# A transformer layer on one core: deviations inverted in pairs, the first unit's scores in the projection, and extra products in attention's lead

## The chip, the cores and the metric

The kernel runs on one core of a Trainium2 chip. The metric is the time of one execution in microseconds (us), the median of several runs. Every time of the trace comes from one profiled execution; positions in it are us from the start of its span. TensorE is PE (its weight loads PEld), VectorE DVE, ScalarE ACT, GpSimd POOL and SyncE SP.

## What is computed

The reference is one pre-norm layer on x of shape (8, 512, 256), in float32:

```python
x = x + attn(layernorm(x))          # 16 heads of 16, scores + relative position bias, softmax
x = x + ffn(layernorm(x))
def ffn(x, ...):
    sh = gelu(xf @ sw1 + sb1) @ sw2 + sb2                 # shared expert, all rows
    logits = xf @ gate_w.T + expert_bias                  # 7 routed experts
    topv, topi = top_k(logits, 2); w = softmax(topv)      # two experts for each row
    h = gelu(einsum('td,edh->eth', xf, rw1) + rb1)
    out_e = einsum('eth,ehd->etd', h, rw2) + rb2
    return sh + einsum('te,etd->td', combine, out_e)
```

## The kernel before

The work stands in three stages, each with a program written out by hand for every engine; the engines meet only at semaphores, and each does its own work strictly in the order written.

**Projection** (`project`, L264). For each of the 8 batches, a slot: PE makes q and k in four groups (pQ, L508, each product in three parts of high and low halves), turns the next batch (pT, L498) and makes v (pV, L519); ACT copies the high half of a group (L459), DVE subtracts it for the low half (L426); SP stores q, k and v to DRAM (L549, L555). After the slots of batches 2 to 5, SP loads one of four tables of the near bias (`near`, L208), and at the very end the first of the attention units (`load_step` of quad 0, place 0: 11 transfers, L229 to L242).

**Attention** (`attend`, L643). A unit is four heads of one batch; there are 32, and a ring of four holds their q and k. For a unit, PE makes 16 blocks of scores (pS, L887, eight steps of two), DVE adds the bias to each and takes the negated maxima (L810, 0.61 us from start to start when it runs without a gap), and turns them (`turn`, L817 to L823). POOL stores the maxima to DRAM and loads them back as rows of q_st (L769, L776). Then PE makes the exponents with bias and maxima in the product (pE, L904, L912), ACT takes Exp (L847), and PE multiplies with the values (pC, L926). Scores run ahead of exponents by one unit and LEAD = 7 steps, so that a lead of 15 steps (L946) stands ahead of the first exponents, on PE alone; from step 1 of the first unit's exponents on, scores of the third unit are asked for. SP loads unit 1, the near bias as bands, then units 2 and 3 (L685 to L689), while ACT's queue stores batch 7 of the projection (L857 to L859).

**Routing and experts** (`finish`, L962). For batch i of 8: PE makes the gate's product (L1632), DVE chooses two experts for a row (`choose`, L1228 on), PE counts the rows before each (`rank`, L1645) and DVE works out the places (`slots`, L1305); POOL scatters the normalised rows to DRAM, 8 indirect transfers for each batch (L1184). Beside it runs the second layernorm of later batches: DVE multiplies the context with the inverse denominators (`context`, L580), PE projects it (`out_projection`, L603), DVE adds the residual and takes statistics (`add_residual`, L613 to L622), POOL inverts the deviation (`invert_deviation`, eight small instructions L256 to L634, for one batch of 4 values in a partition), ACT normalises into `xr` (L1503), PE turns the rows (L1625), ACT copies them (L1511). The shared expert (L1678, L1696) and the splitting of the experts' weights into high and low parts (`weights_hi` L1494, `weights_lo` L1207) fill in. When all rows are scattered, 38 tiles of 256 rows go through their experts (L1706, L1722, L1733), and the results are gathered and added.

```python
for i in range(B):                      # POOL, L1188
    if 2 <= i + 1 < B:
        inverse_deviation(i + 1)
    if i >= 1:
        scatter(i - 1, 1)
    scatter(i, 0)
```

## Time and profile before

| what | us |
|---|---|
| median of 3 runs | 822.09 (820.17 to 823.49) |
| the profiled execution, its own time | 820.95 |
| its span | 819.1 |
| PE busy in the span | 773.4 (94%) |
| PEld busy | 551.9 (67%) |
| DVE busy | 619.1 (76%) |
| ACT busy | 474.8 (58%) |
| POOL busy | 260.6 (32%) |
| granted TensorE clock, mean | 0.958 of full speed |

The span divides by PE's lines: projection to 101.5, attention to about 532, routing to about 661, expert tiles to about 785, and the end. Busy shares are means over stages with different limits; a matmul's end is modelled, so that a busy PE isn't PE at its peak. The granted clock is a share of full speed: 1.00 is 2.4 GHz, 0.50 is 1.2 GHz.

### The profile page before, as it was taken

To read this page: it belongs to the slowest core of one execution; us is meant where nothing else is said; L and a number is where in the kernel's file an instruction comes from. 1 tells how busy PE (TensorE), PEld (TensorE's weight loads), DVE (VectorE), ACT (ScalarE), POOL (GpSimd) and SP (SyncE) were. 2 spreads that over 40 slices of the span, in tenths; PEclk is the share of its full clock that TensorE was granted. 3 is DMA by queue.
4 is the path that set the end of the run, shared out by engine and by line. 5 is a ranking of instruction groups with operands and counts; after the bars stand their busy time and mean duration, and the time that the engine had idled before them with its cause. 6 is when DMAs were issued, how large, how long until landed. Compare 5 with 4: busy or idle time off the path is not lost. (4 is left out here: it accounts for less than half of the span.)

```text
span 819.1 us, 18303 instructions
## 1 busy us (share of the span) xinstructions
PE 773.4 (94%) x6261; PEld 551.9 (67%) x6261; DVE 619.1 (76%) x1928; ACT 474.8 (58%) x716; POOL 260.6 (32%) x407
## 2 busy tenths in 40 slices
PE   4899989999999999999999999998997999999997
PEld 2677737566566566566565665777765589999974
DVE  4666487889889889888888884477865567777966
ACT  2344404766766766666666667466454267777730
POOL 1222111121121111111111111237777526666650
PEclk9999956999999999999999999988897999999999
DMA  4899883553364343453345284466632545556769
GB/s 117 229 351 360 304 259 109 135 145 100 101 170 137 116 123 106 151 169 101 99 121 152 81 267 136 166 187 206 212 101 85 175 133 165 161 158 208 222 202 355
DMA packets 74763, 140.77 MB, mean 172 GB/s; under 512 B 14651, under 2 KB 34771, under 8 KB 74497
## 3 DMA queue, kind: packets, MB, share of 16 engines
q1 hardware_dynamic: 62996, 116.12, 46.1%
q0 software_dynamic: 9792, 19.54, 7.4%
q10 hardware_dynamic: 1884, 3.97, 1.4%
q8 instruction: 50, 0.82, 0.4%
q14 instruction: 41, 0.33, 0.1%
HBM read 85.71 MB, written 56.78 MB: 174 GB/s over the span
## 5 line engine op out<-in xcount | busy, mean ns | idle before, releaser
L810 DVE CUSTOM_DVE_ANT_0 sums<-pS,near 128x512 bf16<-128x512 f32 x512 | 329.4, 688 | 48.4 <-PE pS L887 40.0
L847 ACT ACTIVATE prob<-pE 128x1024 f32<-128x1024 f32 x256 | 248.6, 1022 | 152.9 <-PE pE L912 152.8
L912 PEld LDWEIGHTS pE<-bandT,place 64*128 64x128 f32 x2048 | 167.4, 190 | 12.6
L912 PE MATMUL pE<-bandT,place 64*128 64x244 f32 (+2 forms) x2048 | 164.4, 272 | 0.0
L887 PE MATMUL pS<-k_st,q_st 48*128 48x512 f32 x512 | 139.0, 478 | 6.1 <-DVE nmax L810 2.5
L887 PEld LDWEIGHTS pS<-k_st,q_st 48*128 48x128 f32 x512 | 62.8, 193 | 115.6 <-DVE nmax L810 87.8
L926 PE MATMUL pC<-prob,v_aug 128*32 128x512 f32 x1024 | 135.7, 604 | 0.0
L904 PE MATMUL pE<-q_st,k_st 62*128 62x512 f32 x512 | 115.7, 407 | 1.4 <-issue 1.4
L1199 POOL DMA_INDIRECT expert_rows<-rb,xr x76 | 83.7, 1101 | 57.1 <-DVE rb L1414 45.5
L1184 POOL DMA_INDIRECT routed_rows<-xr,slot_i x64 | 66.2, 1034 | 32.2 <-issue 31.3
L1733 PE MATMUL pD<-w2p,hT 128*128 x456 | 63.5, 289 | 0.4 <-DVE hT L1407 0.4
L776 POOL DMA_DIRECT2D q_st<-negated_maxima x64 | 34.9, 550 | 89.9 <-DMA negated_maxima<-turned 89.9
L904 PEld LDWEIGHTS pE<-q_st,k_st 62*128 62x128 f32 x512 | 57.7, 189 | 6.9 <-ACT prob L847 4.2
L785 POOL COPY v_aug<-v_raw 128x256 f32<-128x256 f32 x32 | 12.7, 398 | 151.3 <-PE pC L926 151.3
L1733 PEld LDWEIGHTS pD<-w2p,hT 128*128 128x128 f32 x456 | 56.8, 190 | 0.7 <-issue 0.6
L769 POOL DMA_DIRECT2D negated_maxima<-turned x32 | 22.6, 706 | 92.3 <-DVE turned L823 88.2
L508 PE MATMUL pQ<-xT,w_p 128*128 128x512 f32 x192 | 48.9, 405 | 3.2 <-DVE qk L426 2.5
L1407 DVE TENSOR_TENSOR hT<-ctx_sb,hT 128x512 fp32r<-128x512 f32 x38 | 26.3, 693 | 28.3 <-ACT hT L1560 28.3
L508 PEld LDWEIGHTS pQ<-xT,w_p 128*128 128x128 f32 x192 | 35.7, 193 | 15.5 <-DVE qk L426 6.5
L810 DVE DVE_READ_ACCUMULATOR2_ANT nmax<- 128x1 f32 x512 | 42.7, 83 | 0.0
L926 PEld LDWEIGHTS pC<-prob,v_aug 128*32 128x32 f32 x1024 | 20.4, 108 | 31.2 <-issue 30.4
L459 ACT ACTIVATE qk<-pQ 128x512 fp32r<-128x512 f32 x32 | 19.2, 599 | 31.6 <-PE pQ L508 27.3
(202 smaller groups left out, 1066.7 us busy)
## 6 DMA issues: line engine op xcount, KB each, us to landing
xr<-routed_rows SPq DMA_DIRECT2D x38, 258.0 KB, 2.9
q_st<-q_parts SPq DMA_DIRECT2D x64, 128.0 KB, 2.7
k_st<-k_parts SPq DMA_DIRECT2D x64, 128.0 KB, 2.9
ctx<-ctx_sb SPq DMA_DIRECT2D x32, 256.0 KB, 2.7
q_parts<-qk SPq DMA_DIRECT2D x14, 512.0 KB, 7.8
k_parts<-qk SPq DMA_DIRECT2D x14, 512.0 KB, 7.4
near<-bias_by_distance SPq DMA_DIRECT2D x16, 448.0 KB, 5.0
xr<-expert_rows SPq DMA_DIRECT2D x14, 512.0 KB, 4.3
```

What stands on the lines that cost most here:

```text
L508: ins = pe.matmul(pQ[:, m % 2], w_p[:, a, w, c, P * h:P * h + P], xT[:, par, z, c], start=k == 0, stop=k == 5)
L776: pool.dma_start(raw(q_st[row:row + KM, m % RING]), max_dram[m].rearrange("a (p h) s -> h a p s", h=2)[side]).then_inc(max_ld, 16)
L810: dve.tensor_tensor_reduce(sums[:, r % 4], pS[:, unit % PS], near[:, hg % 2, j, lead:lead + S], -1.0, BIG, ALU.add, ALU.min, nmax[:, j, t: ...
L847: act.activation(prob[:, par, 2 * step:2 * step + 2], pE[:, 2 * (step % 2):2 * (step % 2) + 2], ACT.Exp).then_inc(exp_done, 1)
L887: pe.matmul(pS[:, unit % PS], q_st[rows, r, pair, P * t:P * t + P], k_st[rows, r, pair], start=True, stop=True).then_inc(s_mm, 1)
L904: pe.matmul(pE[:, bank + side], k_st[rows, r, pair, P * t:P * t + P], q_st[rows, r, pair], start=True, stop=False, skip_group_check=True)
L912: ins = pe.matmul(pE[:, bank + side, a:z], place[rows, half], bandT[rows, (quad // 2) % 2, pair, part, lead:lead + z - a], start=False, st ...
L926: ins = pe.matmul(pC[32 * j:32 * j + 32], v_aug[:, par, t, j], prob[:, par, at], start=t == 0, stop=t == TT - 1, skip_group_check=True)
L1184: pool.indirect_dma_start(xs_dram[:, :], bass.IndirectOffsetOnAxis(ap=slot_i[:, b, c, t:t + 1], axis=0), xr[:, b % XR, t, c], None).then_i ...
L1199: pool.indirect_dma_start(yc_dram[:, :], bass.IndirectOffsetOnAxis(ap=place_of, axis=0), y_rows(i)[:, t], None).then_inc(y_out[i % NXG], 16)
L1407: dve.tensor_tensor(hT[:, i % 2, 1], h_f[:, i % 2], hT[:, i % 2, 0], ALU.subtract).then_inc(s["hlo"], 1)
L1733: ins = pe.matmul(pD[:, i % 2, t], hT[:, i % 2, a, TS * m + P * t:TS * m + P * t + P], w2p[:, bass.ds(expert, 1), z, m].rearrange("p a n - ...
```

## The change

It has three parts. In the projection, the tables of the near bias are loaded one slot earlier (after batches 1 to 4), unit 0 is loaded after batch 5's stores and unit 1 at the end, both before attention begins. In the last slot, batch 7's, PE makes the 16 blocks of unit 0's scores between its own groups, two at a time, into the two banks of pB, and DVE takes their maxima between the low halves and after them. Attention then starts with `turn(0)` on DVE, and PE's lead has seven steps, each followed by two products of `ident` with itself into pC, which nobody reads. In the routing, one inversion serves two batches (2 and 3, 4 and 5, 6 and 7), at every second batch and between two halves of a scatter; the out projections, residuals, contexts and parts of the weights are done in pairs too, and in other places of the engines' orders.

```diff
-        mv = sb("mv2", [P, TT, 2], F32)
-        half = sb("half2", [P, TT], F32)
-        rtmp = sb("rtmp2", [P, 2, TT], F32)
-        rstd = sb("rstd2", [P, 2, TT], F32)
-        nbias = sb("nbias", [P, 2, TT], F32)
+        mv = sb("mv2", [P, 2, TT, 2], F32)
+        half = sb("half2", [P, 2, TT], F32)
+        rtmp = sb("rtmp2", [P, 2, 2, TT], F32)
+        rstd = sb("rstd2", [P, 4, TT], F32)
+        nbias = sb("nbias", [P, 4, TT], F32)
...
                 for b in range(B - 1):
                     slot(b, b % 2, b // 2, b < B - 2)
                     if b < 2:
                         load_rows(b)
-                    elif b < 2 + HPG:
-                        if b == 2:
-                            wait_apart(sp, passed, bias_stored, 16 * (4 + FARS))
-                        loads["near"](sp, 0, b - 2)
-                for m in range(4):
-                    wait_apart(sp, passed, qk_out[m], 16 * (B - 2))
-                wait_apart(sp, passed, v_out, 16 * (B - 2))
-                loads["step"](sp, 0, 0, True)
+                    if b == 1:
+                        wait_apart(sp, passed, bias_stored, 16 * (4 + FARS))
+                    if 1 <= b < 1 + HPG:
+                        loads["near"](sp, 0, b - 1)
+                    if b == 1 + HPG:
+                        stored(B - 4)
+                        loads["step"](sp, 0, 0, True)
+                stored(B - 2)
+                loads["step"](sp, 0, 1, True)
...
+                        if not one:
+                            maxima(m)
...
+                def maxima(step):
+                    pair, t = divmod(step, TT)
+                    for side in range(2):
+                        unit, j = 2 * step + side, 2 * pair + side
+                        if t == 0:
+                            dve.wait_ge(g["near_ld"][j], 16)
+                        dve.wait_ge(g["s_mm"], unit + 1)
+                        if unit >= 4:
+                            dve.wait_ge(g["max_done"], unit - 3)
+                        lead = P * t
+                        dve.tensor_tensor_reduce(g["sums"][:, unit % 4], pB[:, unit % 2], g["near"][:, 0, j, lead:lead + S], -1.0, BIG,
+                                                 ALU.add, ALU.min, g["nmax"][:, j, t:t + 1]).then_inc(g["max_done"], 1)
...
+                for step in range(4, 2 * TT):
+                    maxima(step)
...
+                def scores(step):
+                    pair, t = divmod(step, TT)
+                    if step == 0:
+                        pe.wait_ge(g["qk_ld"][0], 16 * 8)
+                        pe.wait_ge(bias_done, 2)
+                    for side in range(2):
+                        unit = 2 * step + side
+                        rows = slice(HALF * side, HALF * side + KQ)
+                        if unit >= 2:
+                            pe.wait_ge(g["max_done"], unit - 1)
+                        pe.matmul(pB[:, unit % 2], g["q_st"][rows, 0, pair, P * t:P * t + P], k_st[rows, 0, pair],
+                                  start=True, stop=True).then_inc(g["s_mm"], 1)
...
+                            scores(m)
...
+                            if u == 1:
+                                ins.then_inc(v_mm, 1)
+                            if not one:
+                                scores(4 + t)
...
+def inverses_until(b):
+
+    return b + 1 if b < 2 else 2 + b // 2
...
+        dve.wait_ge(s["var2"], 4 * b)
+    if b >= 2:
+        dve.wait_ge(s["rstd2d"], inverses_until(b - 2))
...
-def invert_deviation(pool, g, b):
-
-    s, mv, rstd, nbias = g["early"], g["mv"], g["rstd"][:, b % 2], g["nbias"][:, b % 2]
-    pool.wait_ge(s["var2"], 4 * b + 4)
-    _, ins = rsqrt_steps(pool, g["passed"], mv, g["half"][:], rstd, g["rtmp"], s["chain2"], 7 * b)
+def invert_deviation(pool, g, batches):
+
+    s, b, count = g["early"], batches[0], 7 * (inverses_until(batches[0]) - 1)
+    part, rows = slice(b % 2, b % 2 + len(batches)), slice(b % 4, b % 4 + len(batches))
+    mv, rstd, nbias = g["mv"][:, part], g["rstd"][:, rows], g["nbias"][:, rows]
+    half, tmp = g["half"][:, part], g["rtmp"]
+    pool.wait_ge(s["var2"], 4 * batches[-1] + 4)
+    _, ins = rsqrt_steps(pool, g["passed"], mv, half, rstd, tmp[:, :, part], s["chain2"], count)
     ins.then_inc(s["chain2"], 1)
-    pool.wait_ge(s["chain2"], 7 * b + 6)
-    pool.tensor_tensor(nbias, mv[:, :, 0], rstd, ALU.mult).then_inc(s["chain2"], 1)
-    pool.wait_ge(s["chain2"], 7 * b + 7)
+    pool.wait_ge(s["chain2"], count + 6)
+    pool.tensor_tensor(nbias, mv[:, :, :, 0], rstd, ALU.mult).then_inc(s["chain2"], 1)
...
-                loads["step"](sp, 0, 1, True)
...
+                turn(0)
+                for ahead in range(STEPS, STEPS * NI):
...
-                for step in range(STEPS + LEAD):
-                    scores(step // STEPS, step // STEPS, 1, step % STEPS)
+                for step in range(LEAD):
+                    scores(1, 1, 1, step)
+                    for _ in range(2):
+                        pe.matmul(pC[:, 0:P], g["ident"][:], g["ident"][:], start=True, stop=True)
...
-                    if i + 4 < B:
-                        sp.wait_ge(s["wo_mm"], 2 * (i + 2) + 2)
-                        load_context(sp, g, i + 4)
+                    for b in (i + 4, i + 5):
+                        if i % 2 == 0 and b < B:
+                            sp.wait_ge(s["wo_mm"], 2 * (b - 2) + 2)
+                            load_context(sp, g, b)
...
-                def inverse_deviation(b):
-                    pool.wait_ge(s["xn2"], 4 * (b - 2) + 4)
-                    invert_deviation(pool, g, b)
-
-                def scatter(b, c):
+                def inverse_deviations(pair):
+                    if pair[0] >= 4:
+                        pool.wait_ge(s["xn2"], 4 * (pair[0] - 3) + 4)
+                    invert_deviation(pool, g, pair)
+
+                def scatter(b, c, tokens=range(TT)):
                     if b == 0:
                         pool.wait_ge(pad_out[1], 16)
                     pool.wait_ge(s["slot_done"], b + 1)
                     pool.wait_ge(s["meta_done"], 2 * b + 2)
                     pool.wait_ge(s["xn2"], 4 * b + 4)
-                    for t in range(TT):
+                    for t in tokens:
                         pool.indirect_dma_start(
                             xs_dram[:, :], bass.IndirectOffsetOnAxis(ap=slot_i[:, b, c, t:t + 1], axis=0),
                             xr[:, b % XR, t, c], None).then_inc(scat[b % XR], 16)
 
                 for i in range(B):
-                    if 2 <= i + 1 < B:
-                        inverse_deviation(i + 1)
-                    if i >= 1:
+                    if i % 2 == 1 and i + 2 < B:
+                        scatter(i - 1, 1, range(2))
+                        inverse_deviations((i + 1, i + 2))
+                        scatter(i - 1, 1, range(2, TT))
+                    elif i >= 1:
                         scatter(i - 1, 1)
...
+                context(dve, g, 3)
                 dve.wait_ge(s["consts"], 7 + NE)
                 for i in range(B):
-                    if 1 <= i < B - 1:
-                        residual(i + 1)
-                    if i >= 3 and i % 2 == 1:
-                        add((i - 3) // 2)
                     choose(i)
-                    if i < B - 1:
-                        shares_and_places(i)
                     if i == 0:
                         dve.wait_ge(s["den_ld"], 16)
                         dve.reciprocal(den[:], den[:]).then_inc(s["den_inv"], 1)
-                    if i < B - 1:
-                        running(i)
-                        slots(i)
-                    else:
-                        running(i)
-                        slots(i)
-                        shares_and_places(i)
-                    if i + 3 < B:
-                        context(dve, g, i + 3)
-                    if i < NR:
-                        for k in (2 * i, 2 * i + 1):
+                    running(i)
+                    slots(i)
+                    shares_and_places(i)
+                    if i % 2 == 0:
+                        for b in (i + 2, i + 3):
+                            if b < B:
+                                residual(b)
+                    elif i >= 3:
+                        add((i - 3) // 2)
+                    rounded = (2 * i - 2, 2 * i - 1, 2 * i, 2 * i + 1) if i % 2 == 1 else (2 * i, 2 * i + 1)
+                    if i in (1, 3, 5, NR - 1):
+                        for k in rounded:
                             weights_lo(k)
+                    if i % 2 == 1:
+                        for b in (i + 3, i + 4):
+                            if b < B:
+                                context(dve, g, b)
...
-                        act.wait_ge(s["rstd2d"], b + 1)
+                        act.wait_ge(s["rstd2d"], inverses_until(b))
...
                         normalise(i + 1, 0)
+                    if i + 1 < B:
+                        turned(i + 1)
                     if i % 2 == 1:
                         shares(i // 2)
-                    if i + 1 < B:
-                        turned(i + 1)
                     if i < NR:
                         for k in (2 * i, 2 * i + 1):
...
                     if i % 2 == 1:
                         shared_up(i // 2, 0)
                         shared_up(i // 2, 1)
-                        if i < B - 1:
-                            turn_shares(i // 2)
-                    elif i >= 2:
-                        shared_down(i // 2 - 1, (0,))
-                    if i + 2 < B:
-                        out_projection(i + 2)
+                    else:
+                        if i >= 2:
+                            shared_down(i // 2 - 1, (0,))
+                        if i + 2 < B:
+                            out_projection(i + 2)
                     rank(i)
                     if i + 1 < B:
                         turn_rows(i + 1)
-                    if i % 2 == 0 and i >= 2:
-                        shared_down(i // 2 - 1, (1,))
+                    if i % 2 == 1:
+                        if i < B - 1:
+                            turn_shares(i // 2)
+                    else:
+                        if i >= 2:
+                            shared_down(i // 2 - 1, (1,))
+                        if i + 3 < B:
+                            out_projection(i + 3)
                 turn_shares(EARLY)
                 pe.wait_ge(s["tab_chain"], 3 * B)
                 pe.matmul(pX[:, 1, 0, 0:2 * NE], ones_b[:], cum[:, B], start=True, stop=True).then_inc(s["cnt_mm"], 1)
```

How the orders change shows at three places. PE, from the last slots of the projection to the first exponents (pQ and pV are the projection's, pB and pS scores, pC the values' bank, pE exponents; L5.. lines of `project`, L8.. or L9.. of `attend`). Before:

```order
L519 MATMUL pV<-w_p,xT 128x256 x24
L508 MATMUL pQ<-xT,w_p 128x512 x24
L519 MATMUL pV<-w_p,xT 128x256 x24
L308 UNCONDITIONAL_BRANCH
L873 UNCONDITIONAL_BRANCH
L887 MATMUL pS<-k_st,q_st 128x512 x32
L904 MATMUL pE<-q_st,k_st 128x512 x2
```

The 16 blocks of unit 0 and 16 of the later ones stand in one run behind the projection (30 of the lead and 2 of the first step). Now:

```order
L561 MATMUL pV<-w_p,xT 128x256 x24
L548 MATMUL pQ<-xT,w_p 128x512 x6
L538 MATMUL pB<-k_st,q_st 128x512 x2
...
L561 MATMUL pV<-w_p,xT 128x256 x6
L538 MATMUL pB<-k_st,q_st 128x512 x2
L312 UNCONDITIONAL_BRANCH
L927 UNCONDITIONAL_BRANCH
L941 MATMUL pS<-k_st,q_st 128x512 x2
L1003 MATMUL pC<-ident 128x128 x2
...
L941 MATMUL pS<-k_st,q_st 128x512 x2
L958 MATMUL pE<-q_st,k_st 128x512 x2
```

Unit 0's blocks went into the last slot, a pair behind each of its eight groups (four of pQ, four of pV), and seven pairs with the extra products are what is left of the lead.

POOL, from the first scatters of the routing on (L256 to L634, now L260 to L689, are one inversion). Before:

```order
L1184 DMA routed_rows<-xr,slot_i 60928x258 x4
L256 TENSOR_SCALAR rtmp<-mv 128x4
L257 TENSOR_TENSOR rstd<-rtmp,half 128x4
L258 TENSOR_TENSOR rtmp<-rstd 128x4
L259 TENSOR_TENSOR rtmp<-rtmp 128x4
L260 TENSOR_SCALAR rtmp<-rtmp 128x4
L261 TENSOR_TENSOR rstd<-rstd,rtmp 128x4
L632 TENSOR_TENSOR nbias<-mv,rstd 128x4
L634 TENSOR_SCALAR nbias<-nbias 128x4
L1184 DMA routed_rows<-xr,slot_i 60928x258 x8
```

An inversion of 4 values stands ahead of every 8 scatters, six times. Now:

```order
L1242 DMA routed_rows<-xr,slot_i 60928x258 x6
L260 TENSOR_SCALAR rtmp<-mv 128x8
L261 TENSOR_TENSOR rstd<-rtmp,half 128x8
L262 TENSOR_TENSOR rtmp<-rstd 128x8
L263 TENSOR_TENSOR rtmp<-rtmp 128x8
L264 TENSOR_SCALAR rtmp<-rtmp 128x8
L265 TENSOR_TENSOR rstd<-rstd,rtmp 128x8
L687 TENSOR_TENSOR nbias<-mv,rstd 128x8
L689 TENSOR_SCALAR nbias<-nbias 128x8
L1242 DMA routed_rows<-xr,slot_i 60928x258 x16
```

Three inversions of 8 values are left, with 16 scatters from one to the next.

PE, from batch 2's gate to batch 3's (gate into pX from ga_f, shared expert's second product into pD, out projection from wo_f, counting from mask, turning from xr). Before:

```order
L1632 MATMUL pX<-ga_f,x2T 128x7 x8
L1694 MATMUL pD<-b2s,cTs 128x256
...
L603 MATMUL pX<-wo_f,cn 128x256 x8
L1645 MATMUL pX<-mask,tri_b 128x64
...
L1625 MATMUL pX<-ident,xr 128x128 x8
L1694 MATMUL pD<-b2s,cTs 128x256
...
L1632 MATMUL pX<-ga_f,x2T 128x7 x8
```

Each batch has one out projection ahead of its count. Now:

```order
L1692 MATMUL pX<-ga_f,x2T 128x7 x8
L1754 MATMUL pD<-b2s,cTs 128x256
...
L648 MATMUL pX<-wo_f,cn 128x256 x8
L1705 MATMUL pX<-mask,tri_b 128x64
...
L1685 MATMUL pX<-ident,xr 128x128 x8
L1754 MATMUL pD<-b2s,cTs 128x256
...
L648 MATMUL pX<-wo_f,cn 128x256 x8
L1692 MATMUL pX<-ga_f,x2T 128x7 x8
```

An even batch has two, and the second stands last, ahead of the next batch's gate; an odd batch has none.

## Rows read from the trace of the kernel before

**Rows 1.** Windows: busy us of each engine (count), granted clock, DMA share, GB/s.

```profile
84.00:88.00 4.00, 3.94 (x18) 2.88 (x17) 2.17 (x7) 1.72 (x3) 2.07 (x6) 1.00 1.08 382
132.00:136.00 4.00, 3.83 (x24) 3.22 (x24) 2.32 (x7) 1.83 (x3) 0.00 (x0) 0.54 0.01 4
544.74:651.00 106.26, 95.89 (x420) 69.32 (x420) 75.28 (x368) 51.96 (x103) 80.63 (x112) 0.86 0.51 158
```

**Rows 2.** Timeline of attention's lead: start, us, engine, line, instruction [idle before <-releaser].

```profile
102.80 0.70 PE L887 MATMUL pS<-k_st,q_st 48*128 48x512 f32 x3 [1.24 <-DVEq L796]
...
113.20 0.08 DVE L810 DVE_READ_ACCUMULATOR2_ANT nmax<- 128x1 f32 x1
...
114.57 0.97 POOL L769 DMA_DIRECT2D negated_maxima<-turned  x1 [10.85 <-DVE turned L823]
...
114.59 1.22 PE L887 MATMUL pS<-k_st,q_st 48*128 48x512 f32 x3 [2.30 <-DMA k_st<-k_parts]
```

**Rows 3.** PE's timeline from the first exponents on.

```profile
123.72 1.01 PE L904 MATMUL pE<-q_st,k_st 62*128 62x512 f32 x2
...
126.41 0.64 PE L887 MATMUL pS<-k_st,q_st 48*128 48x512 f32 x1
...
136.19 0.49 PE L887 MATMUL pS<-k_st,q_st 48*128 48x512 f32 x1 [0.36 <-DVE nmax L810]
...
138.85 0.49 PE L887 MATMUL pS<-k_st,q_st 48*128 48x512 f32 x1 [0.33 <-DVE nmax L810]
```

**Rows 4.** Timeline of the projection's last two slots, SP's queue and ACT.

```profile
85.76 1.72 SPq L549 DMA_DIRECT2D q_parts<-qk  x2
...
94.03 0.64 SPq L229 DMA_DIRECT2D q_st<-q_parts  x1
...
94.24 0.60 ACT L459 ACTIVATE qk<-pQ 128x512 fp32r<-128x512 f32 x1 [0.79 <-PE pQ L508]
...
100.69 0.35 SPq L242 DMA_DIRECT2D v_raw<-v_rows  x1
```

**Rows 5.** Line L549, the stores of q and k.

```profile
DMA to landing us min/median/max: 3.2/7.1/8.4
```

**Rows 6.** Timeline of POOL, the inversion for batch 6 between two scatters, and the last wait.

```profile
591.48 0.96 POOL L1184 DMA_INDIRECT routed_rows<-xr,slot_i  x1 [0.30 <-issue]
...
592.85 1.04 POOL L257 TENSOR_TENSOR rstd<-rtmp,half 128x4 f32<-128x4 f32 x1
...
596.12 1.10 POOL L1184 DMA_INDIRECT routed_rows<-xr,slot_i  x1 [0.51 <-issue]
...
641.44 0.96 POOL L1184 DMA_INDIRECT routed_rows<-xr,slot_i  x1 [1.55 <-issue]
```

**Rows 7.** Timeline of DVE and PE in the routing.

```profile
535.87 6.68 PE L603 MATMUL pX<-wo_f,cn 128*128 128x256 f32 x16
...
587.06 1.28 DVE L613 TENSOR_TENSOR x1c<-pX,x1c 128x512 f32<-128x512 f32 x2
...
597.45 1.22 DVE L580 TENSOR_TENSOR cn<-cn,rb 128x1024 f32<-128x1024 f32 x1
...
599.12 1.13 PE L1696 MATMUL pD<-w_sh,ctx_sb 128*128 128x256 f32 x4
...
600.72 0.69 DVE L1207 TENSOR_TENSOR w2p<-wst,w2p 128x512 fp32r<-128x512 f32 x1
...
608.81 4.00 PE L603 MATMUL pX<-wo_f,cn 128*128 128x256 f32 x16
...
619.77 0.15 DVE L1228 TENSOR_TENSOR logits<-pX,eb 128x28 f32<-128x28 f32 x1
...
624.73 0.17 DVE L1313 CAST slot_i<-slot_f 128x8 int32<-128x8 f32 x1
```

**Rows 8.** Chain that ended last, in order of time: start, us, what.

```profile
650.87 4.52 DMA routed_rows<-xr,slot_i
...
660.94 0.66 PE pX L1706 x4
```

30 lines of the change are left out of this document (18 added, 12 removed).

## Prediction

> **What bounds the kernel now.** I read the windows first, for the clock and for the engine that is never free; then the timeline of attention's lead and of the projection's last slots; then POOL's timeline and the chain of waits in the routing. The windows show two weak places. At 132 to 136 PE is granted 0.54 of its clock, though attention has long begun, and in the routing, from 544.7 to 651, it has 0.86 on average [rows 1]. In the same 106.3 us POOL is busy for 80.6, more than its neighbour DVE (75.3), and what is left is mostly a gap of 0.30 that stands ahead of each scatter [rows 1, 6]: POOL sets the pace. The chain says the same: from the last scatter at 650.87 it goes through the DMA to PE's first tiles at 660.94 [rows 8]. In the lead the order is: first scores at 102.80, the last maximum of unit 0 at 113.20, its store to DRAM at 114.57, PE's wait of 2.30 for unit 1's k until 114.59, the first exponents at 123.72 [rows 2, 3]. In between, attention has nothing for ACT and little for PE. The steady part of attention (to about 530) and the expert tiles (from 661) are PE's; the change doesn't touch them, so what is won ahead of them shifts them whole.
>
> **Part 1: unit 0's scores in the last slot of the projection.** Nothing is removed: 16 blocks go from the lead into batch 7's slot. DVE carries it. It gets its first low half there at about 94.9, behind ACT's copy at 94.24 [rows 4]; from then on it has four low halves (a subtraction of 128x512 takes 0.69 [rows 7]) and 16 maxima at a cadence of 0.61 (16 of them fill most of 102.80 to 113.28 [rows 2]), so 2.8 + 9.8 = 12.6 us: 107.5. PE feeds it with two banks instead of three and has to make its own groups between; I add 1 us: 108.5. Between stages PE stood idle for about 1.3 before 102.80 [rows 2]; so `turn(0)` comes at 109.8 instead of behind 113.28: 3.5 us earlier. PE's part is hidden by DVE's: 16 blocks of 512 columns beside some 9 us of its own groups.
>
> What the moved load does to SP's queue: unit 0's eleven transfers, issued from 94.03 to 101.04 [rows 4], now stand from about 84 to 91, ahead of the stores of batch 6's q and k, which before were issued from 85.76. These become about 5 us late. Batch 7's first copy overwrites a buffer that such a store reads; it ran at 94.24, and a store takes 7.1 us to land in the median, 3.2 at least [rows 4, 5]. So 91.1 plus 3.2 to 7.1 gives 94.3 to 98.2: a stall of 0 to 4 us in the last slot. The DMA engines are full there (share 1.08 [rows 1]), but unit 0's megabyte replaces a table of the near bias, and I take 1 us. The Trainium skill ("Trainium Kernel Development and Optimization", Key Constraints) says that transfers issued from SP, ACT and POOL all run on the same 16 engines and interleave. By that rule the early load delays the stores even on another queue; it is the fourth case below. The tables of the near bias, each one slot earlier, cost nothing: the number in front of loads of x stays about the same.
>
> Unit 1 is now loaded by about 105, in the projection, so the wait of 2.30 and the 1.3 until the first block's maximum go, and the lead is 14 blocks: 110.8 + 0.7 for `turn` + 8.5 = 120. Late next is unit 2, which PE asks for one step behind the first exponents (126.41 before [rows 3]). Its transfers stand at attention's start, behind the bands, beside batch 7's stores on ACT's queue. Unit 1 stood just so before and took from about 102.5 to 114.59, 12.1 us [rows 2]; from 110.8 that gives 122.9, at which PE goes on instead of at 126.4. **Part 1 is worth -3** (ends: 0, where the stall is 4; -5.5, where neither costs).
>
> **Part 2: the products that nobody reads.** 14 products of 128 columns, on PE alone, and PE waits there for DVE: cover is DVE's 1.22 per pair of blocks. At full clock an out product of 256 columns is two records, 4.00/16 = 0.25 each [rows 7], so one of these is at most 0.5 us; two of them and two blocks fit 1.22 about exactly. At the low clock they don't, and the lead grows by at most 0.6 per step, 4 us in all. What they can bring: the first three pairs of steps, from 123.72 to 136.19, took 12.5 us, 4.16 each, at about half of the clock (0.54 at 132 to 136) [rows 1, 3]; the next pair, at full clock, took 2.66 [rows 3]. Held at 2.4 GHz they save 4.5 us. PE had fallen behind two gaps and a stretch in which it had one block in 0.61 us. Now it is busy in most of each step, but the gap between the stages stays, with nothing in it. I take that the clock falls there and is back within the lead or by the first pair: **-3** (ends: -4.5 and +1.5, where it stays low and the products lengthen the lead).
>
> **Part 3: the routing.** An inversion costs POOL 596.12 - 591.48 - 1.27 (a scatter with its gap) = 3.4 us [rows 6]. Six are 20.4. A paired one runs the same eight instructions on 8 values. The pow takes 1.04 on 4 [rows 6]; on 8 it takes 1.04 to 2.08. I take 1.8, as a slow function on so little data is nearer to work than to overhead: 4.2 an inversion, three are 12.6. -7.8 for the three. (64 scatters of 1.27, the six inversions and the last wait make 103.0 of the 106.3; the other 3.3 are scatters that took longer, 0.05 each.) The wait of 1.55 at 641.44 [rows 6], for the shares of the last batch behind ACT and PE, goes with it, as DVE will be well ahead of POOL by then: -1.3. POOL's own bound is so -9.1. The Trainium skill ("GPSIMD Engine Reference", Performance versus the Vector engine) gives 2.6 cycles per element and core for two inputs. By that rule four more values cost nothing that shows, and the bound would be 2.3 lower, -11.4; the row of 1.04 for 4 values already speaks against taking it for the pow.
>
> But the pair ties the engines into a longer round. Statistics of batch i+3 (i even) release the inversion; then normalising, turning, copying, and the weights' parts, which were 601.4 - 595.6 = 5.8 after an inversion's end [rows 6, 7]; the copy of the shares, 0.6, now lies inside; then the second context of the pair, 1.2 [rows 7]; then PE: out projection 4.0, count 0.3, turning 1.1, half of the shared expert 2.7 (two of 1.37), out projection 4.0 = 12.1 [rows 7], during which DVE does choosing and places (624.9 - 619.8 = 5.1) and one residual (1.3 and 1.8 of statistics); last the second half's residual and statistics, 2.4 [rows 7]. 4.2 + 0.3 + 5.8 + 0.6 + 1.2 + 12.1 + 2.4 = 26.6 us for two batches, beside 25.3 of POOL's (16 x 1.32 + 4.2) and 27.9 before (16 x 1.32 + 6.8). The first such statistics, of batch 3, come when the second out projection of batch 0 is done: 535.87 + 6.68 [rows 7], 1.5 for count and turning, a wait of 1.8 for the first residual, 4.0, 2.4: 552.3. Two rounds later it is 605.5 for batch 7; then 4.2 of inversion and 26 scatters of 1.32: 644.0, against 651.8 before. The rounds need full clock. PE will stand idle in each for about 3 us behind an odd batch's shared expert, where it waits for the inversion; what idleness can cost shows at 535.87, behind the stage's change: 6.68 for an out projection instead of 4.00 [rows 7]. I give each round 1.5 us for it: 647.0. **Part 3 is worth -5** (ends: -9, or -11 by the skill's rule; 0, where a round takes 30.5). Weights and contexts in pairs cost DVE nothing new; SP's loads of weights 4 to 7 wait for the parts of batch 1 until about 561, and are wanted from 570. After the last scatter, PE's own rest ended at about 659.7 and DMA released the first tiles; both move, PE's by more, as its program of the eight batches ends earlier.
>
> **Sum.** -3 - 3 - 5 = -11 on the profiled execution's 820.95: 809.95. The median of the runs is 1.1 higher: **811.0**.
>
> **Rivals.** (a) The forecast, 805 to 815: 0.58. (b) The rounds take 29 to 31, since PE runs at 1.2 GHz in half of them; part 3 brings -3 to +1, the lead's -6 stays: 815. For it: 0.86 in the routing [rows 1]. Against: POOL's gap. 0.16. (c) POOL's bound is met, the clock is held and no stall comes: -4.5 - 4.5 - 9 = -18: 804. 0.10. (d) The change doesn't do what it says in the lead: stores of batch 6 late by 4, the clock falls at the stage's change and the products lengthen the lead; 0 + 1.5, and part 3 with -4: 819.5. 0.12. (e) Slower, by one mechanism: the clock in the rounds. If PE is at 1.2 GHz for all of them, two out projections cost 2 x 2.7 more, and half of the shared expert up to 2.7: 34.7 a round, and the last scatters end at 605.5 + 2 x 8.1 + 38.5 = 660.2, 8.4 later than before; with a lead that brings -2 that is +6.4: 828.5. It decides once a round is over 31. Against: rows of the routing show both lengths. 0.04.
>
> A measurement of this kernel can tell about 0.5%, 4 us, from no change. Faster by more than that (below 818): (a), (b), (c) and a little of (d), 0.85; within it 0.11; slower 0.04. The range is 803 to 819.
>
> **What would show it.** Right: the first exponents by 120 and PE past unit 2's first scores by 123; the clock at 1.00 in the pairs behind them; three inversions of about 4.2; scatters ending near 647; batch 7's first copy no later than 97. Wrong: exponents at 123 or later, a second stretch at 0.5 in the lead, POOL waiting for statistics by more than 4 us in a round.

## The result and the profile after

The change made the kernel slower: 830.71 us in the median of 20 runs (826.18 to 834.09) beside 823.28 (818.09 to 830.06) for the kernel before, a ratio of 1.009 with a 95% interval of 1.0069 to 1.0111. The forecast was 811.0, with 803 to 819 as its range. Runs of either kernel differ by 8 to 12 us among themselves, which will matter below.

The profiled execution took 829.28 us, 8.33 more than the one before. Two marks divide it: the first gate product of the routing (L1692 after, L1632 before) and PE's turning of the first expert tile (L1766, L1706).

| stretch | before | after | difference | forecast |
|---|---|---|---|---|
| span's start to first gate | 533.70 | 535.39 | +1.7 | -6 |
| first gate to first tile | 125.9 | 133.1 | +7.2 | -5 |
| first tile to the end | 159.5 | 158.8 | -0.7 | 0 |

**The lead.** Windows of the changed kernel, with the columns of [rows 1]:

```profile
107.00:112.00 5.00, 3.94 (x18) 2.43 (x17) 4.08 (x14) 1.15 (x2) 0.00 (x0) 1.00 0.00 2
112.00:117.00 5.00, 4.51 (x17) 3.07 (x18) 3.68 (x12) 0.00 (x0) 1.99 (x4) 0.68 0.77 250
117.00:122.00 5.00, 5.00 (x18) 3.01 (x17) 3.35 (x12) 0.00 (x0) 1.53 (x3) 0.50 1.05 356
122.00:127.00 5.00, 4.72 (x20) 3.29 (x20) 3.84 (x11) 0.00 (x0) 0.00 (x0) 0.50 1.00 220
...
132.00:137.00 5.00, 4.63 (x33) 4.09 (x32) 2.53 (x8) 2.69 (x3) 1.50 (x3) 0.50 0.72 162
137.00:142.00 5.00, 4.18 (x43) 3.33 (x41) 4.13 (x13) 3.35 (x4) 0.00 (x0) 0.93 0.07 16
```

And its timeline, which answers to [rows 2, 3]:

```profile
96.76 0.69 DVE L436 SCALAR_TENSOR_TENSOR qk<-pQ,qk 128x512 fp32r<-128x512 f32 x1 [3.40 <-ACT qk L486]
...
111.17 0.69 DVE L455 CUSTOM_DVE_ANT_0 sums<-pB,near 128x512 bf16<-128x512 f32 x1
...
112.16 4.70 SPq L218 DMA_DIRECT2D bandT<-bias_parts_by_distance  x4
...
112.49 0.51 PE L941 MATMUL pS<-k_st,q_st 48*128 48x512 f32 x2 [1.55 <-DVEq L849]
...
113.73 0.96 POOL L822 DMA_DIRECT2D negated_maxima<-turned  x1 [0.32 <-POOL v_aug L816]
...
119.97 1.12 POOL L829 DMA_DIRECT2D q_st<-negated_maxima  x2 [5.27 <-DMA negated_maxima<-turned]
...
126.02 0.80 PE L958 MATMUL pE<-q_st,k_st 62*128 62x512 f32 x2 [0.28 <-DMA q_st<-negated_maxima]
```

The last slot ends with DVE's last maximum at 111.8, not at 108.5. Its first low half came at 96.76, not at 94.9, since PE began the slot's products of q and k at 94.54 instead of 92.66. The DMA engines moved nothing from 107 to 112 (share 0.00) and were full from 117 to 127 (1.05, 1.00): batch 7's stores, the bands and units 2 and 3 are issued by attention, which now begins at 112.2 instead of 102.5. The maxima of unit 0, whose store is issued at 113.73, need 12.3 us to DRAM and back; before it was at most 9.2, as PE did not wait for them there [rows 2, 3]. PE stood idle for 1.55 at the change of stages and has 0.50 of its clock by 117, until about 137; before, it had its full clock back at about 136 [rows 3].

**The routing.** POOL's timeline: each inversion now does two batches, and there are three in the rounds.

```profile
554.09 0.25 POOL L260 TENSOR_SCALAR rtmp<-mv 128x8 f32<-128x8 f32 x1 [1.25 <-DVE mv L674]
554.42 1.67 POOL L261 TENSOR_TENSOR rstd<-rtmp,half 128x8 f32<-128x8 f32 x1
...
585.12 0.26 POOL L260 TENSOR_SCALAR rtmp<-mv 128x8 f32<-128x8 f32 x1 [1.03 <-DVE mv L674]
...
616.15 0.25 POOL L260 TENSOR_SCALAR rtmp<-mv 128x8 f32<-128x8 f32 x1 [1.02 <-DVE mv L674]
...
654.55 0.96 POOL L1242 DMA_INDIRECT routed_rows<-xr,slot_i  x1 [0.30 <-issue]
```

They start 31.03 us apart, twice. What fills a round is seen in PE's timeline from the end of one:

```profile
587.62 0.22 PE L1711 MATMUL pX<-mask,ones_b 128*128 128x48 bf16 x3
591.05 1.40 PE L1685 MATMUL pX<-ident,xr 128*128 128x128 f32 x8 [3.21 <-ACT xr L1563]
592.24 1.06 PE L1729 MATMUL pD<-ident,combine_p 128*24 128x128 f32 x4
593.09 3.42 PE L1692 MATMUL pX<-ga_f,x2T 128*128 128x7 f32 x16
596.44 0.58 PE L1754 MATMUL pD<-b2s,cTs 24*128 24x256 f32 x1
596.95 2.08 PE L1756 MATMUL pD<-w_sh,ctx_sb 128*128 128x256 f32 x4
...
601.33 4.14 PE L648 MATMUL pX<-wo_f,cn 128*128 128x256 f32 x16
...
608.68 1.13 PE L1756 MATMUL pD<-w_sh,ctx_sb 128*128 128x256 f32 x4
609.64 3.89 PE L648 MATMUL pX<-wo_f,cn 128*128 128x256 f32 x16
613.38 1.85 PE L1692 MATMUL pX<-ga_f,x2T 128*128 128x7 f32 x16
```

PE waits 3.21 for the normalised rows, and what follows runs at half of the clock: the gate's product takes 3.42, and 1.85 later in the round; four products of the shared expert 2.08, and 1.13 later. Added up, the rows at half clock from 592.24 on cost some 4.6 us more than the same products at full clock. Apart from that one wait PE is hardly ever free in a round. The chain that ended last, which before ran from a scatter through the DMA into the tiles [rows 8], now runs over PE, with one piece of DVE at 644.86, to the end of the stretch:

```profile
638.83 3.54 PE pU L1738 x8
...
658.03 3.43 PE pU L1738 x8
...
666.96 1.73 PE pU L695 x8
```

Behind the rounds PE meets a wait that the kernel before doesn't have, for DVE's addition of the shared expert's rows, which the change puts behind the choosing and the places of an odd batch:

```profile
646.29 1.01 PE L1729 MATMUL pD<-ident,combine_p 128*24 128x128 f32 x4 [3.81 <-DVE x1c L1384]
```

### The profile page after: what moved, and what is told of

The parts are those of the page before. It is cut to its first block and busy times, and to the rows that moved or that the text cites. A ratio compares the mean times of both kernels' runs of the same rounds, so it can differ in the third digit from the quotient of the medians.

```text
span 827.3 us, 18329 instructions
## 1 busy us (share of the span) xinstructions
PE 778.9 (94%) x6289; PEld 559.3 (68%) x6289; DVE 620.3 (75%) x1928; ACT 474.7 (57%) x716; POOL 253.3 (31%) x383
## 5 line engine op out<-in xcount | busy, mean ns | idle before, releaser
L863 DVE CUSTOM_DVE_ANT_0 sums<-pS,near 128x512 bf16<-128x512 f32 x496 | 319.9, 688 | 47.1 <-PE pS L941 38.9
L941 PE MATMUL pS<-k_st,q_st 48*128 48x512 f32 x496 | 127.3, 469 | 3.1 <-DVE nmax L863 1.6
L941 PEld LDWEIGHTS pS<-k_st,q_st 48*128 48x128 f32 x496 | 57.4, 190 | 104.3 <-DVE nmax L863 77.7
L548 PE MATMUL pQ<-xT,w_p 128*128 128x512 f32 x192 | 50.6, 413 | 2.6 <-DVE qk L436 2.2
L486 ACT ACTIVATE qk<-pQ 128x512 fp32r<-128x512 f32 x32 | 19.1, 598 | 34.7 <-PE pQ L548 28.0
```

Source lines behind the costliest of these rows:

```text
L548: ins = pe.matmul(pQ[:, m % 2], w_p[:, a, w, c, P * h:P * h + P], xT[:, par, z, c], start=k == 0, stop=k == 5)
L863: dve.tensor_tensor_reduce(sums[:, r % 4], pS[:, unit % PS], near[:, hg % 2, j, lead:lead + S], -1.0, BIG, ALU.add, ALU.min, nmax[:, j, t: ...
L941: pe.matmul(pS[:, unit % PS], q_st[rows, r, pair, P * t:P * t + P], k_st[rows, r, pair], start=True, stop=True).then_inc(s_mm, 1)
```

## The experiments

### The two halves of the change

`e1` has the lead's part alone, `e2` the routing's part alone.

> The kernel before with the lead's part of the change alone (unit 0's scores in the projection's last slot, the earlier loads, two products behind each pair of the lead's scores); the routing as it was. Theory: the lead's part loses by itself, by what the changed kernel shows at the stage's end. First exponents at about 126.0 instead of 123.7, the routing's first work at 535.4 instead of 533.7, total +1.7 us (ratio 1.002). Rival: the 1.7 us are lost again in attention's slack or in the rounds, ratio 1.000. Second rival: the lead's part is a gain that the routing's part hides, ratio below 0.997.

> The kernel before with the routing's part alone (inversions in pairs, and the orders on DVE, PE, ACT, SP and POOL that belong to it); projection and attention as they were. Theory: a round for two batches takes 31.0 us again, since PE's own row of work in it fills it, wherever it starts: total +5.5 to +7, ratio 1.007 to 1.009. Rival: the rounds are long because they begin 1.7 us late, against loads of weights that don't move; then they come out nearer to 28 and the ratio near 1.000.

Measured: lead alone 1.0009 (0.9971 to 1.0047), routing alone 1.0114 (1.0068 to 1.016). In its profile the lead alone brings the first gate to 535.62 (1.9 late), the routing alone has its inversions at 554.59, 585.61 and 616.62: 31.02 and 31.01 apart though its lead is the old one. So the loss is the routing's, and a round's length is its own and not that of a late start. The lead's part is no gain in total. The first gate can't price it: in the four profiles with the old lead it lies anywhere from 531.30 to 538.99 (535.83 in `e2`), so the 1.7 of the first table is no measure of the lead.

An earlier mark can. POOL's fifth copy of v from the start of attention (`v_aug<-v_raw`) lies ahead of attention's second half and of the routing, where executions differ most:

| lead | profiles | fifth copy of v |
|---|---|---|
| old | before, e2, e5, e10 | 175.88, 174.11, 172.89, 175.40 |
| changed | changed, e1, e4, e6, e9 | 178.41, 178.79, 179.82, 176.20, 179.49 |
| changed, no products | e3 | 180.03 |
| transfers earlier (below) | e11, e12, e13, e14 | 176.21, 174.57, 176.61, 175.01 |

All five profiles of the changed lead are later than all four of the old one, by 4.0 us in the mean. The total of `e1` is compatible with that (the upper end of its interval is 3.9 us) and with nothing.

### The lead without its products

```diff
                 for step in range(LEAD):
                     scores(1, 1, 1, step)
-                    for _ in range(2):
-                        pe.matmul(pC[:, 0:P], g["ident"][:], g["ident"][:], start=True, stop=True)
```

> The lead's part alone, without its 14 products that nobody reads. Theory: PE's clock falls at the change of stages in any case, and at half of it the products cost 7 x 0.6 us in the lead's 7 steps; without them a step is bound by DVE's 1.22 us, the first exponents come at about 121.5 instead of 126.0, the low clock still ends at about 137, total 3 to 4 us below the lead's part with them, ratio to the kernel before about 0.997. Rival: the products hold up the clock's return; without them the half clock lasts longer than 137.6, and the 4 us are lost again in the pairs of steps (4.2 us at half clock, 2.7 at full), ratio about 1.002.

Measured: 1.0024 (0.999 to 1.0059). Its number is the rival's; what happened is neither theory. In this execution attention began 2.8 us later than in the changed kernel, PE was at half clock from 107 on, and then this happened:

```profile
116.56 0.97 POOL L811 DMA_DIRECT2D negated_maxima<-turned  x1 [0.32 <-POOL v_aug L805]
...
122.81 1.12 POOL L818 DMA_DIRECT2D q_st<-negated_maxima  x2 [5.29 <-DMA negated_maxima<-turned]
...
128.93 0.80 PE L947 MATMUL pE<-q_st,k_st 62*128 62x512 f32 x2 [3.93 <-DMA q_st<-negated_maxima]
```

PE was done 3.93 us early and waited for the maxima, which took 12.4 us again. The products cost nothing that shows in the changed kernel, since the maxima's way hides them (PE waited 0.28 for them there): a bound that I had not priced at all.

### PE's idle stretch in a round, filled with products

```diff
                     rank(i)
+                    if i % 2 == 1 and i + 1 < B:
+                        keep_turning(pe, g, pX[:, 0, 1, 0:D], 7)
                     if i + 1 < B:
                         turn_rows(i + 1)
```

> The changed kernel with seven products of 256 columns that nobody reads in each round, in the 3.2 us in which PE waits for an even batch's normalised rows. Theory: the rounds are long because PE, idle there, is granted 1.2 GHz for the 8 us behind it (gate 3.2 instead of 1.85, half of the shared expert 5.0 instead of 2.75, out projection 4.1 instead of 3.9). With the gap filled the clock stays, a round is 31.0 - 3.8 = about 27 us, the last scatter ends some 10 us earlier, total 8 to 11 us below the changed kernel: ratio to the kernel before about 0.998. Rival: PE's clock in the rounds does not depend on that gap; the products then run at half clock, end behind the rows' arrival, and a round becomes longer, up to 33: ratio 1.014.

Measured: 0.9943 (0.9914 to 0.9972), 821.12 us: 1.5 points below the changed kernel's ratio, by 21 products whose results nothing uses. The theory held, with a gain larger than the 8 to 11 us expected (about 12 by the ratios). PE's timeline at the place shown above:

```profile
566.31 2.08 PE L1756 MATMUL pD<-w_sh,ctx_sb 128*128 128x256 f32 x4
...
585.43 3.27 PE L695 MATMUL pX<-wo_f,ident 128*128 128x256 f32 x14
588.77 1.09 PE L1685 MATMUL pX<-ident,xr 128*128 128x128 f32 x8
589.70 0.60 PE L1729 MATMUL pD<-ident,combine_p 128*24 128x128 f32 x4
590.14 1.93 PE L1692 MATMUL pX<-ga_f,x2T 128*128 128x7 f32 x16
...
592.31 1.13 PE L1756 MATMUL pD<-w_sh,ctx_sb 128*128 128x256 f32 x4
```

The gate's product is back at 1.93. Inversions start at 554.91, 582.85 and 609.22: rounds of 27.9 and 26.4 instead of 31.0 twice. In the first of them, four products of the shared expert still took 2.08 at 566.31, though PE had not waited since 546.76; only the second ran at full clock throughout. Nothing else differs between the two kernels, so the clock behind the gap is shown to be what lengthens a round: 4.6 us of it. The wait behind the rounds is left, at 3.75.

`e5` does the like to the kernel before:

```diff
                     if i + 1 < B:
+                        keep_turning(pe, g, pX[:, 0, 1, 0:D], 2)
                         turn_rows(i + 1)
```

> The kernel before, with two products of 256 columns that nobody reads ahead of each batch's turning in the routing, where PE waits 0.8 to 1.3 us (once 4.1). Theory: in the order of before POOL sets the pace of the rounds and PE's half clock is hidden; ratio 0.998 to 1.002, whatever the clock does. Rival: the gain of the held rounds was the clock's alone and has nothing to do with pairs; then the same comes here, 4 us or more, ratio 0.995 or less.

Measured: 1.0017 (0.9981 to 1.0053), no gain. But the reason I gave, that the clock is hidden there, isn't borne out. Its profile spends 135.9 us from first gate to first tile, at a clock of 0.77, with idle stretches left that the products don't fill (4.45 ahead of a turning at 596.52, 2.21 at 629.89). So a kernel before whose clock is held was not made, and how much of the later gains the pairs themselves bring stays open. Four profiles have the old order of the rounds, and by and large the longer ones have the lower clock (the routing of `e7` and `e8` begins 12 to 15 us later than the changed kernel's, so that their window lies earlier in it):

| kernel | rounds | clock at 560 to 650 | first gate to first tile |
|---|---|---|---|
| before | old | 0.84 | 125.9 |
| e1 | old | 0.75 | 133.1 |
| e3 | old | 0.85 | 125.4 |
| e5 | old, products | 0.77 | 135.9 |
| changed | pairs | 0.81 | 133.1 |
| e2 | pairs | 0.79 | 136.0 |
| e14 | pairs | 0.81 | 133.2 |
| e4 | pairs, held | 0.91 | 123.7 |
| e6 | pairs, filled | 0.87 | 122.0 |
| e7 | pairs, held | 0.94 | 123.1 |
| e8 | pairs, held | 0.98 | 120.4 |
| e9 | pairs, tuned | 0.94 | 120.7 |
| e10 | pairs, tuned | 0.91 | 120.6 |
| e11 | pairs, tuned | 0.92 | 119.6 |
| e12 | pairs, tuned | 0.94 | 116.6 |
| e13 | pairs, tuned, held | 0.92 | 118.8 |

In the old order the clock falls at places that differ from one execution to the next; in pairs with the gap it falls behind the gap in every round of all three profiles (least in the first round of `e14`, which took 29.3).

### Real work in the gap

PE's part of the edit; ACT's copy of the shares also goes ahead of the normalising, and DVE's addition of the shared expert's rows ahead of the choosing:

```diff
...
-                    else:
-                        if i >= 2:
-                            shared_down(i // 2 - 1, (0,))
-                        if i + 2 < B:
-                            out_projection(i + 2)
+                    elif i + 2 < B:
+                        out_projection(i + 2)
                     rank(i)
+                    if i % 2 == 1 and i < B - 1:
+                        turn_shares(i // 2)
+                        shared_down(i // 2, (0,))
```

> The changed kernel; in the gap of 3.2 us in each round stands the work that PE now does behind it, the turning of the shares and the first half of the shared expert (0.6 + 2.75 us at full clock), instead of products that nobody reads; ACT copies the shares ahead of the normalising, DVE adds the shared expert's rows ahead of choosing. Theory: the round is bound by PE's row of work and by its clock; the gap is gone, the clock stays, and 3.3 us less work follows it: a round of 25 to 26 us (POOL's own bound is 25.3) instead of 31.0 in the changed kernel and 26.4 to 28.0 in the held one. Total 3 to 6 us below the held one, ratio to the kernel before 0.987 to 0.991. Rival: the moved copy and addition stand in the way of normalising or choosing, the gap opens again and the clock falls: ratio 1.000 or more.

Measured: 0.9957 (0.9922 to 0.9992): better than the changed kernel by 1.3%, no better than the held one. Rounds of 27.2 and 29.4, not 25 to 26. Two small waits had come in, 0.88 for the copy of the shares and 1.5 for an even batch's context, and in the second round the out projection behind the latter took 6.56. The wait of 3.8 behind the rounds is gone with DVE's earlier addition, and the first tile now waits 0.43 for the DMA: in this kernel and its successors not only the gap differs from the change. `e9` mends both small waits; `e10` is the same with the old lead.

```diff
-                    elif i + 2 < B:
-                        out_projection(i + 2)
+                    else:
+                        if i >= 2:
+                            shared_down(i // 2 - 1, (1,))
+                        if i + 2 < B:
+                            out_projection(i + 2)
...
                         turn_shares(i // 2)
+                        keep_turning(pe, g, pX[:, 0, 1, 0:D], 2)
                         shared_down(i // 2, (0,))
```

> The filled rounds with their two small gaps closed as well: the second half of the shared expert now stands ahead of the even batch's out projection (which waited 1.5 us for its context), and two products that nobody reads bridge the 0.8 us in which the copy of the shares is waited for. Lead as in the changed kernel. Theory: where PE has no idle stretch in a round, its clock holds through the routing, as it did not in one of three filled rounds (out projection 6.56 instead of 3.9, 612 to 628 at half): rounds of 26 us each, total 3 to 4 us below the filled rounds, ratio to the kernel before 0.990 to 0.992. Rival: POOL's own 25.3 and DVE's row bind already, and the clock in the routing is hidden: same as the filled rounds, 0.995.

> The same rounds with projection and lead of the kernel before. Theory: the lead's part of the change is worth nothing or a small loss (1.0009, interval 0.9971 to 1.0047, measured alone), so this comes 0 to 2 us below the same rounds with the new lead. Rival: the new lead gains where the rounds no longer bind: 1 to 3 us above.

Measured: 0.9889 (0.9836 to 0.9943) and 0.9901 (0.9867 to 0.9935), 818.33 and 817.6 us. The stretch is 120.7 and 120.6, against 122.0. The totals came about as expected, but the rounds did not come to 26: 27.7 and 30.2 in the first. One wait of 1.7 is left, ahead of the second out projection, which takes 5.3 to 5.6 behind it. The leads can't be told apart by the totals, as with the lead's part alone.

### The lead: transfers earlier, and a bridge

`e7` and `e8` issue batch 7's stores, the bands and units 2 and 3 from SP within the projection; the rounds are the held ones. The lines added there (and taken out of attention):

```diff
                 loads["step"](sp, 0, 1, True)
+                for m in range(4):
+                    wait_apart(sp, passed, qk_lo, 4 * (B - 1) + m + 1)
+                    store_qk(sp, g, B - 1, m)
+                for j in range(HPG):
+                    loads["band"](sp, 0, j)
+                wait_apart(sp, passed, v_done, 2 * B)
+                store_v(sp, g, B - 1)
+                for r in range(2, RING):
+                    loads["step"](sp, 0, r, True)
```

> The held-rounds kernel (changed kernel with products in the rounds' gap), whose stores of batch 7, band tables and loads of units 2 and 3 are issued in the projection's stage, behind unit 1's load, instead of at attention's start. Theory: the lead fails because those transfers now all begin at 112.2, when the stage changes: the DMA engines' share is 0.46 at 100 to 115 and 1.01 at 115 to 127, and the maxima of unit 0 take from 113.7 to 126.0 to go to DRAM and back. With them spread the way back takes 6 to 8 us, and the exponents wait for the lead's own work at half clock, which ends at about 125: gain 1 us, ratio to the kernel before about 0.993. Rival: the maxima's way is long by itself (two transfers of small pieces, 12 us however idle the DMA engines are); exponents at 126 as before, no gain.

> The same with early transfers, without the lead's 14 products. Theory: with the maxima's way short, the lead's own length counts, and without the products it is DVE's, 10 us instead of 12.5: exponents at 122 to 122.5, total 3.5 us below the held-rounds kernel, ratio to the kernel before 0.989 to 0.991. Rival: without the products the clock stays low for longer, and exponents that begin earlier run at half clock until the same time as before: no gain over the kernel with the products.

Measured: 1.0106 (1.0074 to 1.0138) and 1.0089 (1.0055 to 1.0123), 10 us worse than the held rounds by the medians. The exponents begin at 140.87 and 135.42. Both theories missed what the edit does: SP's row of issues now belongs to the projection's stage, and the stages change when it is through. In `e7`:

```profile
127.06 0.11 POOL L819 MEMSET half<- 128x8 f32 x1 [37.64 <-POOLq L312]
...
128.41 0.96 POOL L827 DMA_DIRECT2D negated_maxima<-turned  x1 [0.32 <-POOL v_aug L821]
```

The one thing they show of the question: with the DMA engines freer, in `e8` (share 0.27 at 128 to 135), the maxima issued at 127.56 had come back by 135.42, in at most 7.9 us. So `e11` leaves units 2 and 3 in attention, puts the stores of q and k on ACT and the bands and v on SP; `e12` adds the bridge, and one product per pair of the lead's scores.

```diff
+                    if not one:
+                        for m in range(4):
+                            act.wait_ge(qk_lo, 4 * b + m + 1)
+                            store_qk(act, g, B - 1, m)
...
                 slot(B - 1, 1, False)
+                for _ in range(6):
+                    pe.matmul(pT[:, 0, 0:P], ident[:], ident[:], start=True, stop=True)
```

> The tuned rounds with the changed kernel's lead without its products; batch 7's stores of q and k on ACT and its store of v and the band tables on SP, inside the projection's stage; loads of units 2 and 3 as in the changed kernel, in attention. The earlier try put all of them on SP, whose row of issues then ended at 127 and held the stage's change from 112 to 127. Theory: the stage changes at 112 to 113, the maxima of unit 0 go to DRAM and back in 8 us (7.7 in that try, 12.3 in the changed kernel), exponents begin at 122 to 123 instead of 126: 3 us below the tuned rounds with the new lead. Rival: SP's row or the full DMA engines hold the stage's change again, gain 0 or a loss.

> The same with six products that nobody reads at the end of the projection's PE row, where PE stood idle for 1.5 us at the change of stages, and one instead of none behind each pair of the lead's scores. Theory: the idle stretch at the stage's change is what lowers the clock at 114; with it bridged the lead runs at 2.4 GHz and the first pairs of steps take 2.7 instead of 4.2 us: 4 us below the same without bridge. Rival: the clock falls for the low load of the lead itself (a pair of scores in each 1.22 us), bridge or not: no gain, or 1 us lost.

Measured: 0.9907 (0.987 to 0.9945), 818.84 us, and 0.9841 (0.9794 to 0.9887), 811.85 us. `e11` missed its theory: instead of 3 us below the tuned rounds (818.33) it is level with them. Exponents begin at 123.82 and 123.69, 2.2 and 2.3 us earlier than in the changed kernel but no earlier than in the kernel before (123.72); the way of the maxima is 8.8 and 9.2. Windows of `e12`:

```profile
112.00:117.00 5.00, 4.40 (x20) 2.53 (x19) 3.84 (x16) 0.00 (x0) 1.99 (x4) 1.00 0.93 254
117.00:122.00 5.00, 5.00 (x15) 2.77 (x14) 4.46 (x15) 0.00 (x0) 1.53 (x3) 0.55 0.95 176
122.00:127.00 5.00, 4.75 (x27) 3.64 (x27) 3.08 (x11) 1.37 (x2) 0.70 (x1) 0.50 0.85 163
...
132.00:137.00 5.00, 4.61 (x48) 3.86 (x48) 4.68 (x15) 3.17 (x5) 0.00 (x0) 1.00 0.02 4
```

In `e12`, bridge and single products together, the clock falls behind 117 instead of ahead of it (1.00 from 112 to 117, in place of 0.68 in the changed kernel and 0.81 in `e11`); the first pairs still run at half. By the fifth copy of v its lead is 1.6 us ahead of `e11`, and inside the range of the old one. The two intervals overlap. The rest of the 7 us between the medians I can't give to the bridge: of the 13.7 between the two spans, 7.1 lie in attention's second half (units 24 to 30 took 81.3 in `e11`, 74.2 in `e12`, 75.3 in the kernel before) and 3.0 in the routing (119.6 and 116.6), where the two programs don't differ.

`e13` has two products for each pair of scores and three in the last gap of the rounds; `e14` has the lead of `e12` with the rounds of the change.

```diff
                         if i + 3 < B:
+                            keep_turning(pe, g, pU[:, 0, 0:D], 3)
                             out_projection(i + 3)
```

> The tuned rounds with early transfers and the bridge at the stage's change, two products behind each pair of the lead's scores, and three products of 256 columns in the gap of 1.7 us that is left in each round ahead of the second out projection. Theory: every idle stretch of PE above 1 us is a chance for the clock to fall; in the tuned rounds the second out projection still took 5.4 to 5.6 us in three profiles. With the gap filled it takes 3.9 and a round 26 us: 2 to 4 us below the bridged kernel's 811.85, ratio to the kernel before 0.980. Rival: those products run where the clock had already fallen, and only lengthen the row: 812 to 814, ratio 0.984.

> The changed kernel with early transfers, the bridge and one product per pair of the lead's scores, its rounds as they are. Theory: the lead is repaired by itself: exponents at 123.7 instead of 126.0 and full clock from 132 instead of 138, so 3 to 4 us below the changed kernel, ratio to the kernel before 1.004 to 1.006; the rounds take 31.0 us again, as their idle stretch is still there. Rival: the 7 us by which the bridged kernel beat the one without bridge came from the lead: ratio 1.001 or below.

Measured: 0.9838 (0.9787 to 0.989), 813.18 us, no different from `e12`, as its rival said; and 1.0061 (1.0029 to 1.0094), 829.19 us. `e14` has the ratio that was expected, and a routing of 133.2 as in the changed kernel, with rounds of 29.3 and 31.0. Its exponents came at 125.61 and not at 123.7: the maxima took 10.1 us here, at a DMA share of 1.08 from 117 to 122, and PE waited 1.17 for them. Its interval overlaps the changed kernel's; that its lead is the better one rests on the fifth copy of v. In `e13` the clock held through the lead, and then this came:

```profile
117.00:122.00 5.00, 5.00 (x28) 3.56 (x26) 5.00 (x17) 0.00 (x0) 1.52 (x3) 1.00 1.01 174
122.00:127.00 5.00, 2.78 (x27) 2.33 (x26) 2.66 (x11) 0.91 (x1) 0.70 (x1) 0.89 0.83 162
127.00:132.00 5.00, 4.63 (x29) 3.42 (x27) 2.80 (x9) 2.52 (x4) 1.49 (x3) 0.50 0.51 135
```

```profile
125.03 0.50 PE L963 MATMUL pE<-q_st,k_st 62*128 62x512 f32 x2 [2.22 <-DMA q_st<-negated_maxima]
```

PE was through with the lead early, waited 2.22 for the maxima (10.1 us again), and the clock fell there instead. In its rounds the second out projection took 4.08 twice behind waits of 0.45, and yet a first one took 4.99. Products in the lead can't bring anything while the maxima's way is its bound.

The best of all, `e12`, is 1.6% faster than the kernel before and, by the two ratios, 2.5% faster than the change; `e13` is its equal. `e10`, with the lead of before, has 0.9901 (0.9867 to 0.9935): what the repaired lead adds to the tuned rounds is not told apart from nothing.

## Why the prediction was wrong

**Part 3 failed at its clock term.** The step was "I give each round 1.5 us for it". The round without it was forecast at 26.6; the round of `e4` that ran at full clock took 26.4. What was wrong is the price of "about 3 us behind an odd batch's shared expert, where it waits for the inversion". The wait was there, at 3.2, and its price is 4.6 us in a round (31.0 less 26.4), three times the 1.5; by the other round of `e4`, where the clock fell once more, 3.1. I had taken it from one out projection (6.68 for 4.00), but the reduced clock covers some 8 us of PE's row: turning of shares, gate, half of the shared expert, which I had left out of what stands behind the gap. That the 26.6 fits is in part luck: behind the normalised rows the sum goes over weights' parts, the copy of the shares and a context, 7.6 us from the inversion's end to the out projection, and in `e4` it is PE's own row that fills this place (turning, gate and half of the shared expert end at 594.65, 8.0 behind the inversion's end). The same term was missing ahead of the first round: the second out projection of the stage, counted with 4.0, took 5.59 behind a wait of 1.69, and the first inversion came at 554.09 instead of 552.3. Rival (b) named the mechanism and the length, 29 to 31, with 0.16. It gave 815 since it kept the lead's -6.

**"Both move, PE's by more", of the first tiles, was wrong.** PE's rest came 9 us later, not earlier (first tile at 668.52, 659.61 before), while the last scatter was issued only 3.7 later (654.55, 650.87 before). With rounds bound by PE, its row behind the last counting is what the tiles wait for. That row takes 26 us from 642.2, where before it took 21 from 639: the wait of 3.81 for DVE's addition is new, a cost of the new order that no term of the sum had. POOL's saving of three inversions (3.8 each, forecast 4.2) was real and worth nothing. "POOL sets the pace" was too strong for the kernel before as well: two batches took 28.1 and 29.1 there, and other profiles of the same order are 7 to 10 us longer at a lower clock. One execution's rounds, by the table one of the two shorter of four, were taken for the kernel's.

**Part 1 failed at two steps.** "I add 1 us: 108.5" for two banks instead of three: PE and DVE alternate in the last slot, and it took 15.1 us from DVE's first low half where 13.6 were forecast: 2.5 instead of the 1. And the tables of the near bias, "each one slot earlier, cost nothing": slots 6 and 7 began 1.6 and 1.9 us later. In all twelve profiles with the new order of loads slot 7 begins between 94.08 and 95.70, in the four with the old one between 92.17 and 93.44. The loss comes with that order; what in it costs the time was not tried. Together they put the end at 111.8, and `turn(0)` at 112.28 instead of 109.8. The stall that I priced at 0 to 4 did not come. Not in the sum at all was that the earlier lead leaves behind attention's own transfers, so that the DMA engines idle and are then full while the maxima need them. The Trainium skill ("Trainium Kernel Development and Optimization", Key Constraints) says that DMAs issued from the SP, ACT and POOL queues all run on the same 16 engines and interleave. The traces agree: the maxima, issued from POOL, took 12.3 us while SP's and ACT's transfers kept the share at 1.0, and at most 7.9 in `e8`. I had applied the rule to batch 6's stores, and not to the transfer on which the exponents wait.

**Part 2** was forecast at -3 with the clock back "within the lead or by the first pair". It fell at about 114 and was back at about 137, one us later than before. The products didn't hold it and cost nothing that shows. When it comes back differs by execution, with either lead: between 122 and 127 in `e5` (old), behind 142 in `e9` (changed). The fourth case (d) described this lead; it had 0.12 and was joined to a routing that gains 4.

**Rival (e)**, slower, asked for rounds of 34.7 and decided "once a round is over 31". The result is slower at 31.0 because the lead brought no -2, and because PE's rest, not the last scatter, set the tiles.

## What to carry to other kernels

Where an order ties several engines into a round, look for the place at which PE waits in every round, and price what follows it at half of the clock, over all of PE's row until it is full again, and not one instruction. Fill such a place with PE's own later work and close what small waits this opens; products that nobody reads did as well here before the small waits were closed, and show in one run whether the clock is the cause. When work is moved ahead of a stage's change, move its transfers too, or they pile up behind it (here even that only brought the lead back to where the old one was); and before holding the clock in a lead, make sure that no transfer is what ends it.

## What was not expected of the hardware

- A wait of PE of 1.55 to 3.2 us, with full work around it, was followed by 8 us (rounds) to 23 us (lead) at 0.50. Behind waits of 1.5 to 1.8 this came in most cases and not in all (in the tuned rounds one out projection took 5.3 to 5.6, in others 4.08).
- A wait is not needed for it. In `e4` four products took 2.08 at 566.31, some 20 us behind PE's last wait, and 2.07 at 620.23, where the last wait was one of 0.41 at 599.07; the same four take 1.13 at full clock. What else lowers it was not looked into.
- The pow on POOL took 1.04 us on 4 values in a partition [rows 6] and 1.67 on 8. The Trainium skill ("GPSIMD Engine Reference", Performance versus the Vector engine) gives about 2.6 cycles per element for `tensor_tensor`, with an addition as its case. By that, as an estimate, the four more would not show; for the pow the trace disagrees, by 0.63.
- Six units in attention's second half took 74 to 81 us in three profiles whose programs don't differ there. The cause was not looked into.
